# Attention and projection kernel: one query tile projected a step earlier, its key tile spread over slots, and the first value burst one exponential later

## Chip, core and metric

The kernel runs on one core of a Trainium2 chip. The metric is the device time of one execution in microseconds (us); lower is better. Engine names are those of the profile: PE is TensorE's matmuls, PEld its weight loads, DVE is VectorE, ACT is ScalarE, POOL is GpSimd, SP is the engine that issues most of the transfers. ACTq and SPq are the transfers that ACT and SP issue.

## What is computed

There are 16 batches of 512 tokens with 512 features. The first layer is softmax attention with 16 heads of 32 features, the second a linear attention with 8 heads. The change is in the first:

```
xn = layer_norm(x)
q = (xn @ q_w + q_b).reshape(16, 512, 16, 32);  k, v likewise
att = softmax_over_keys(einsum('bnhl,bmhl->bnmh', q, k) + mask)
y = einsum('bnmh,bmhl->bnhl', att, v)
x = x + silu(layer_norm(y) * (1 + scale) + shift) @ out_w + out_b
```

## The kernel before

`attention_phase` does the first layer up to y, `projection_phase` (untouched) all that follows. Attention takes the first 1580 us of the span, in 16 batches of four **steps**. Step g of a batch attends for head group g (four heads, 128 features). A step has 16 **slots** (SLOTS), and the order of work in a slot is written out by hand for each engine, in a function `step` of its own; the engines meet only over semaphores.

What a slot holds on PE, in this order:

1. `exp_scores` (L521), one 100x512 product of scores with keys on the partitions, into one of two `exp_bank`s. ACT takes the exponential of it into `probs` (`exp`, L745). The exponentials run LAG = 3 slots late: slot k of step g does exponential k-3 of this step, slots 0 to 2 do exponentials 13 to 15 of the step before. Product e waits until ACT has done exponential e-2.
2. After product e == 5 (slot 8) stands **burst 1**: `weigh_values` 2 and 3 of the step before (L532) and `sum_probs` (L546). After e == 8 (slot 11) stands **burst 2**: `weigh_values` 0 and 1 of this step. ACT copies y out (`copy_y`) after its exponential 5.
3. `max_scores` (L506), a 98x512 product for the next step into one of two `max_bank`s, whose row maximum DVE reduces into `negmax` (`maximum`, L879). 16 of them stand in slots 0 to 10: one in an even slot, two in an odd one, the second at the slot's end (`maxima`). Maximum m waits until DVE has reduced m-2.
4. Between a slot's first and second maximum, one **quarter** of a projected tile (`project_quarter`, L489: three 128x512 products), or four transposes of x (`transpose_x`, L496) in step 1. QUARTERS gives the slots: q in 0 to 3, k in 4 to 7, the first v in 8 to 11, the second in 13 to 15. Steps 0 and 3 have q, k and two v tiles, step 1 has q, k and x in slots 8, 9, 11, 13, step 2 has q and k alone. The q and k tiles are those of two steps on: steps 2 and 3 project groups 0 and 1 of the next batch.
5. In slot 12 the transpose of `negmax` (L512), whose result SP copies into `q_stack` as two shift rows, which exponential product 0 of the next step waits for (`shift_rows`).

When the last quarter of a q or k tile is done, ACT writes its high part (`high_of`, L719) to a stage and issues two transfers of it into the rows of `q_stack` or `k_stack` (`stack_high`, L726). They stand in ACT's order between two exponentials. DVE then makes the low part (`low_of`, L865) one slot later, and SP issues its transfer. Seven transfers a group count up one semaphore `stack_in[g]`, which PE waits for before the group's first maximum, and ACT before it writes the stage again.

Projections and transposes share two `work_bank`s in turn; `take_bank` waits until the use before the last has been read. `uses_of` is the list of uses in a step in their order.

Of the kernel before, what the change touches and what calls it, by code (L numbers as in the profile page):

```python
# [21 lines left out]
F32 = mybir.dt.float32  # L22
# [6 lines left out]
T = 512  # L29
D = 512  # L30
TT = T // P
KT = D // P
DH0 = 32
HG = P // DH0
NG = KT
# [69 lines left out]
def attention_phase(nc, shared, x, mask, mask1, norm_w, norm_b, q_w, q_b, k_w, k_b, v_w, v_b, cond, films, b_vectors,  # L105
# [4 lines left out]
    with ExitStack() as ctx:  # L110
# [83 lines left out]
        hi_done = sem("hi_done")  # L194
        stack_in = [sem(f"stack_in{g}") for g in range(NG)]
        shift_hi, shift_in = sem("shift_hi"), [sem(f"shift_in{g}") for g in range(NG)]
# [9 lines left out]


        def uses_of(g, last):
            u = []
            if not last or g < NG - 2:  # L210
                u += ["q", "k"]
            if g == 0:
                u += ["v2"]
            if g == 1 and not last:
                u += [f"x{tt}" for tt in range(TT - 1)]
            if g == NG - 1 and not last:
                u += ["v0"]
            if not last or g < NG - 1:
                u += ["m"]
            if g == 1 and not last:  # L220
                u += [f"x{TT - 1}"]
            if g == 0:
                u += ["v3"]
            if g == NG - 1 and not last:
                u += ["v1"]
            return u
# [7 lines left out]
        X_TURNS = (8, 9, 11, 13)  # L234
        MAX_TURN = 12

# [20 lines left out]

        def high_count(b, g, i):

            return TT + 4 + HIGHS * b + (2 * g + (TT if g > 1 else 0)) + i + 1  # L260

        STACK_DMAS = 2 * 3 + 1
        HIGH_ROWS = {"q": (0, 2), "k": (0, 1)}
# [27 lines left out]
        def _(sp):  # L291
# [30 lines left out]
            def mask_rows(b, g):  # L322
                sp.dma_start(k_stack[96:98, g, :, :].bitcast(F32),
                             mb_dram[b].unsqueeze(1).broadcast_to([2, HG, T])).then_inc(stack_in[g], DMA)

            def stack_low(n, g):
                sp.dma_start(stack_rows(n, LOW_ROW[n], g), stage[n][:, 1, :].bitcast(F32)).then_inc(stack_in[g], DMA)

# [37 lines left out]
            def step(b, g, last=False, first=False):  # L366
                if not last or g < NG - 2:
                    s_b, s_g = (b, g + 2) if g + 2 < NG else (b + 1, g + 2 - NG)
                    if not (first and g + 2 < NG):

                        sp.wait_ge(exp_full, SLOTS * (step_of(b, g) - 1))
                    mask_rows(s_b, s_g)
                if not last or g < NG - 2:
                    sp.wait_ge(work_read, use(b, g, "q", last)[1] + 1)
                    stack_low("q", s_g)

                if not last or g < NG - 2:
                    sp.wait_ge(work_read, use(b, g, "k", last)[1] + 1)
                    stack_low("k", s_g)
                if not (first and g == 0):  # L380
                    store_y(b, g - 1) if g else store_y(b - 1, NG - 1)
                if g == 0 and not first:
                    store_sums(b - 1)
                if not last or g < NG - 1:
                    n_b, n_g = (b, g + 1) if g + 1 < NG else (b + 1, 0)
                    shift_rows(n_b, n_g, use(b, g, "m", last)[1] + 1)
                if g == 2 and not last and not (type(b) is int and b + 2 >= B):

                    sp.wait_ge(work_full, use(b, 1, f"x{TT - 1}")[1] + 1)
                    load_x(b + 2)  # L390
# [72 lines left out]
        def _(pe):  # L463
# [189 lines left out]
            def step(b, g, last=False, first=False):  # L653
# [3 lines left out]
                for k in range(SLOTS):  # L657
# [10 lines left out]
                    for name, slots in QUARTERS.items():  # L668
                        if name in "qk":
                            if last and g >= NG - 2:  # L670
                                continue
                            what, tile, u = name, (g + 2) % NG, name
                        elif g == 0 or (g == NG - 1 and not last):
                            tile = (2 if g == 0 else 0) + (name == "v'")
                            what, u = "v", f"v{tile}"
                        else:
                            continue
                        for kt in range(KT):
                            if slots[kt] != k:
                                continue  # L680
                            if name == "q" and kt == 0 and g == 2:

                                pe.wait_ge(work_read, use(b, 1, f"x{TT - 1}")[1] + 1)
                            if kt == 0:
                                banks[name] = take_bank(use(b, g, u, last))
                            project_quarter(what, tile, banks[name], kt, kt == 0, kt == KT - 1)
                    if g == 1 and not last and k in X_TURNS:
# [22 lines left out]
        def _(act):  # L710
# [11 lines left out]
            def stack_high(what, g, highs):  # L722

                act.wait_ge(hi_done, highs)
                for row in HIGH_ROWS[what]:
                    act.dma_start(stack_rows(what, row, g), stage[what][:, 0, :].bitcast(F32)).then_inc(stack_in[g], DMA)  # L726

# [51 lines left out]
            for g in range(2):  # L779
                for what in "qk":  # L780
                    if g == 1:
                        act.wait_ge(stack_in[0], DMA * STACK_DMAS)
                    high_of(what, g, n, n)
                    n += 1
                    stack_high(what, g, n)
# [14 lines left out]
            def step(b, g, last=False, first=False):  # L800
                for k in range(SLOTS):
                    if not (first and g == 0 and k < LAG):
                        exp_slot(*exp_of(b, g, k), first and g == 0)
                    for what in "qk":
                        if k == QUARTERS[what][-1] and (not last or g < NG - 2):

                            p_b, p_g = (b, g + 1) if g + 1 < NG else (b + 1, 0)
                            act.wait_ge(stack_in[p_g], DMA * STACK_DMAS * (p_b + 1))
                            static, number = use(b, g, what, last)
                            high_of(what, (g + 2) % NG, number, static)  # L810
                            stack_high(what, (g + 2) % NG, high_count(b, g, "qk".index(what)))
                    if g == 1 and not last and k in X_TURNS:
# [24 lines left out]
        def _(dve):  # L837
# [167 lines left out]
            def step(b, g, last=False):  # L1005
                has_next = not last or g < NG - 1
                n_b, n_g = (b, g + 1) if g + 1 < NG else (b + 1, 0)
                for k in range(SLOTS):
                    if has_next:
                        for m in maxima(k):  # L1010
                            maximum(n_b, n_g, m)
                    for i, what in enumerate("qk"):
                        if k == QUARTERS[what][-1] + 1 and (not last or g < NG - 2):
                            low_of(what, (g + 2) % NG, use(b, g, what, last)[0], high_count(b, g, i))
                    if g == 1 and not last and 5 <= k < 5 + TT:
                        normalise_x(b + 1, [k - 5])
                    if g == 1 and not last and k - 1 in X_TURNS:
                        tt = X_TURNS.index(k - 1)
                        low_of_x(tt, use(b, 1, f"x{tt}")[0], high_count(b, 1, 2 + tt))
                    if k == 11 and (g == 0 or (g == NG - 1 and not last)):  # L1020
# [781 lines left out]
```

## Time and profile before

| | |
|---|---|
| median of 3 runs | 2839.5 us (2839.39 to 2840.51) |
| the profiled execution's own time | 2837.53 us |
| its span, first to last instruction | 2835.7 us |
| PE busy | 2684.1 us (95%) |
| DVE busy | 1822.6 us (64%) |
| ACT busy | 1228.2 us (43%) |
| POOL busy | 1343.5 us (47%) |

PE is the engine that is nearly always busy. Its matmuls are pipelined: a 512-column matmul is shown as about 0.40 us long, while the next starts 0.23 to 0.24 us after it, so durations are read as the distance from start to start. "Idle before" at a row's end is time in which the engine did nothing, and the name behind the arrow is what it waited for. Runs differ by under 0.1%.

### The profile page before, as it was taken

To read this page: it belongs to the slowest core of one execution; us is meant where nothing else is said; L and a number is where in the kernel's file an instruction comes from. 1 tells how busy PE (TensorE), PEld (TensorE's weight loads), DVE (VectorE), ACT (ScalarE), POOL (GpSimd) and SP (SyncE) were. 2 spreads that over 40 slices of the span, in tenths; PEclk is the share of its full clock that TensorE was granted. 3 is DMA by queue.
4 is the path that set the end of the run, shared out by engine and by line. 5 is a ranking of instruction groups with operands and counts; after the bars stand their busy time and mean duration, and the time that the engine had idled before them with its cause. 6 is when DMAs were issued, how large, how long until landed. Compare 5 with 4: busy or idle time off the path is not lost. (4 is left out here: it accounts for less than half of the span.)

```text
span 2835.7 us, 43874 instructions
## 1 busy us (share of the span) xinstructions
PE 2684.1 (95%) x13890; PEld 1951.8 (69%) x13890; DVE 1822.6 (64%) x3276; ACT 1228.2 (43%) x2040; POOL 1343.5 (47%) x598
## 2 busy tenths in 40 slices
PE   6899999999999999999999689999999999999997
PEld 3565566556655665566555468888888888888886
DVE  4666666666666666666665566777676677666673
ACT  2455555555555555555555423333333333333332
POOL 0365655655666565556566323433333333433332
PEclk9999999999999999999999799999999999999999
DMA  7555656665666566656654411111111111111100
GB/s 181 123 95 95 94 80 94 94 96 78 94 97 98 74 97 98 96 78 96 95 83 69 147 35 49 49 49 45 48 49 45 36 46 41 49 49 35 47 30 30
DMA packets 114915, 211.44 MB, mean 75 GB/s; under 512 B 12408, under 2 KB 14508, under 8 KB 114876
## 3 DMA queue, kind: packets, MB, share of 16 engines
q1 hardware_dynamic: 78012, 143.81, 21.7%
q10 hardware_dynamic: 36864, 67.13, 17.8%
q8 instruction: 22, 0.36, 0.1%
q14 instruction: 17, 0.14, 0.0%
HBM read 74.87 MB, written 34.18 MB: 38 GB/s over the span
## 5 line engine op out<-in xcount | busy, mean ns | idle before, releaser
L879 DVE TENSOR_REDUCE negmax<-max_bank 128x1 f32<-128x512 f32 x1024 | 684.5, 687 | 333.6 <-PE max_bank L506 329.4
L745 ACT ACTIVATE probs<-exp_bank 128x512 f32<-128x512 f32 x1024 | 591.9, 596 | 564.2 <-PE exp_bank L521 469.0
L284 POOL TENSOR_TENSOR probs_sum<-probs_sum,probs 128x2048 f32<-128x2048 f32 x126 | 580.6, 4608 | 86.2 <-ACT probs L745 83.8
L284 POOL TENSOR_TENSOR probs_sum<-probs 128x2048 f32<-128x2048 f32 x63 | 287.9, 4570 | 587.0 <-ACT probs L745 587.0
L506 PE MATMUL max_bank<-k_stack,q_stack 98*128 98x512 f32 x1024 | 426.6, 418 | 27.6 <-DVE negmax L879 22.8
L521 PE MATMUL exp_bank<-q_stack,k_stack 100*128 100x512 f32 x1024 | 422.5, 424 | 23.1 <-ACT probs L745 22.5
L506 PEld LDWEIGHTS max_bank<-k_stack,q_stack 98*128 98x128 f32 x1024 | 195.2, 191 | 149.0 <-issue 58.5
L521 PEld LDWEIGHTS exp_bank<-q_stack,k_stack 100*128 100x128 f32 x1024 | 193.6, 190 | 127.6 <-ACT probs L745 73.1
L1500 POOL TENSOR_TENSOR sT_lo<-silu,sT_hi 128x512 fp32r<-128x512 f32 x128 | 172.8, 1370 | 175.8 <-DVE sT_hi L1615 175.8
L532 PE MATMUL y_bank<-probs,v_sb 128*32 128x512 f32 x2048 | 247.7, 602 | 0.0
L1281 PE MATMUL b_work<-ident,area 128*128 128x128 f32 x1536 | 192.8, 281 | 23.8 <-DMA b_sums<-sums_scratch 12.0
L1255 PE MATMUL b_work<-b_wout_hi,sT_hi 128*128 128x512 f32 x512 | 201.7, 394 | 9.6 <-issue 5.1
L1281 PEld LDWEIGHTS b_work<-ident,area 128*128 128x128 f32 x1536 | 175.9, 145 | 37.9 <-DVE area L1584 13.0
L1255 PE MATMUL b_work<-b_wout_lo,sT_hi 128*128 128x512 f32 x512 | 201.1, 393 | 0.0
L1255 PE MATMUL b_work<-b_wout_hi,sT_lo 128*128 128x512 f32 x512 | 200.9, 392 | 0.0
L1495 POOL TENSOR_TENSOR rstd_y<-var_eps_y,b_minus_half 128x4 f32<-128x4 f32 x32 | 32.7, 1022 | 333.6 <-DVE var_eps_y L1579 333.6
L1615 DVE CAST sT_hi<-silu 128x512 fp32r<-128x512 f32 x128 | 102.2, 820 | 103.5 <-ACT silu L1440 103.5
L1479 ACT ACTIVATE area<-area 128x512 f32<-128x512 f32 x64 | 40.4, 632 | 275.0 <-POOL area L1545 275.0
L1440 ACT ACTIVATE silu<-b_work,film_b,film_a 128x512 f32<-128x512 f32 x128 | 93.0, 775 | 128.7 <-PE b_work L1281 101.5
L874 DVE TENSOR_TENSOR v_sb<-work_bank,v_bias 128x512 f32<-128x512 f32 x64 | 44.2, 691 | 153.8 <-PE work_bank L489 153.8
L1515 POOL TENSOR_TENSOR result<-area,row_out 128x512 f32<-128x512 f32 x64 | 83.1, 1308 | 125.2 <-DMA out_x<-result 125.2
L532 PEld LDWEIGHTS y_bank<-probs,v_sb 128*32 128x32 f32 x2048 | 53.7, 109 | 123.6 <-issue 121.1
(203 smaller groups left out, 5308.6 us busy)
## 6 DMA issues: line engine op xcount, KB each, us to landing
q_stack<-q_stage ACTq DMA_DIRECT2D x128, 256.0 KB
k_stack<-k_stage ACTq DMA_DIRECT2D x128, 256.0 KB
x_sb<-in_x SPq DMA_DIRECT2D x16, 1024.0 KB, 5.4
q_stack<-q_stage SPq DMA_DIRECT2D x64, 256.0 KB
k_stack<-k_stage SPq DMA_DIRECT2D x64, 256.0 KB
yT_scratch<-y_stage SPq DMA_DIRECT2D x64, 256.0 KB
area<-yT_scratch SPq DMA_DIRECT2D x16, 1024.0 KB, 5.3
area<-in_x SPq DMA_DIRECT2D x64, 256.0 KB, 2.8
```

The source lines that it names most:

```text
L284: eng.tensor_tensor(probs_sum[:, :, :], so_far, probs[:, mt, :, :], ALU.add).then_inc(probs_added, 1)
L506: pe.matmul(max_bank[m % 2][:, :], q_stack[0:ROWS_MAX, g, j, nt * P:(nt + 1) * P], k_stack[0:ROWS_MAX, g, j, :], start=True, stop=True).th ...
L521: pe.matmul(exp_bank[k % 2][:, :], k_stack[0:ROWS_EXP, g, j, mt * P:(mt + 1) * P], q_stack[0:ROWS_EXP, g, j, :], start=True, stop=True).th ...
L532: last = pe.matmul(y_bank[DH0 * j:DH0 * (j + 1), :], v_sb[:, mt, P * j + DH0 * g:P * j + DH0 * (g + 1)], probs[:, mt, j, :], start=(mt == ...
L745: act.activation(probs[:, mt, j, :], exp_bank[k % 2][:, :], ACT.Exp).then_inc(exp_done, 1)
L879: dve.tensor_reduce(negmax[:, m:m + 1], max_bank[m % 2][:, :], AXX, ALU.max, negate=True).then_inc(max_done, 1)
L1255: last = pe.matmul(out, lhs(a, kt), rhs(c, kt), start=(kt == 0 and a + c == 0), stop=(kt == KT - 1 and a == 1))
L1281: last = pe.transpose(out[:, i * P:(i + 1) * P], src(i), ident[:, :])
L1440: act.activation(silu[:, kt % SILUS, :], bank(u), ACT.Silu, scale=film_columns(film_a[film], kt, row), bias=film_columns(film_b[film], kt, ...
L1500: pool.tensor_tensor(sT_lo[:, kt, :], silu[:, kt % SILUS, :], sT_hi[:, kt, :].bitcast(F32), ALU.subtract).then_inc(sT_lo_done, 1)
L1515: pool.tensor_tensor(result[:, tt, :], x_sb[:, tt, :], rows["out1"][:, :], ALU.add).then_inc(result_biased, 1)
L1615: dve.tensor_copy(sT_hi[:, kt, :], silu[:, kt % SILUS, :]).then_inc(sT_hi_done, 1)
```

## The change

- The second q tile of the next batch (group 1) moves from step 3, slots 0 to 3, to step 2, slots 8 to 11. It is called `q'` there.
- The k tile of group 1 stays in step 3 but has its quarters in slots 0, 2, 4 and 6, where it had 4 to 7.
- `stack_in` becomes a semaphore for each group and each of q and k (3 and 4 transfers). ACT's wait before it writes a stage is for the same letter's tile in the group in front; PE waits for both before a group's first maximum.
- Burst 1, and ACT's `copy_y`, stand behind exponential 6 (slot 9), where they stood behind exponential 5 (slot 8).
- SP issues the low part of `q'` behind the shift rows of step 2. High and low parts follow the last quarter as before: ACT in slot 11, DVE in slot 12, ahead of `split_shift`.

```diff
+        def tiles_of(g, last):
+            return {n: t for n, t in TILES[g].items() if not last or g == 0 or (g == 1 and n in "qk")}
...
+        TILES = [
+            {"q": (2, (0, 1, 2, 3)), "k": (2, (4, 5, 6, 7)), "v2": (2, (8, 9, 10, 11)), "v3": (3, (13, 14, 15, 15))},
+            {"q": (3, (0, 1, 2, 3)), "k": (3, (4, 5, 6, 7))},
+            {"q": (0, (0, 1, 2, 3)), "k": (0, (4, 5, 6, 7)), "q'": (1, (8, 9, 10, 11))},
+            {"k": (1, (0, 2, 4, 6)), "v0": (0, (8, 9, 10, 11)), "v1": (1, (13, 14, 15, 15))},
+        ]
...
-        QUARTERS = {"q": (0, 1, 2, 3), "k": (4, 5, 6, 7), "v": (8, 9, 10, 11), "v'": (13, 14, 15, 15)}
...
-        STACK_DMAS = 2 * 3 + 1
+        STACK_DMAS = {"q": 3, "k": 3 + 1}
...
                 if m == 0:
-                    pe.wait_ge(stack_in[g], DMA * STACK_DMAS * (b + 1))
+                    for n in "qk":
+                        pe.wait_ge(*copied(n, b, g))
...
                 exp_scores(b, g, e, first)
                 before = (b, g - 1) if g else (b - 1, NG - 1)
-                if e == 5 and not first:
+                if e == 6 and not first:
                     weigh_values(*before, 2)
                     weigh_values(*before, 3)
                     sum_probs(*before)
...
                 exp(b, g, e, first)
-                if e == 5 and not first:
+                if e == 6 and not first:
                     copy_y(*((b, g - 1) if g else (b - 1, NG - 1)))
...
-                    for what in "qk":
-                        if k == QUARTERS[what][-1] and (not last or g < NG - 2):
+                    for name, (tile, slots) in tiles_of(g, last).items():
+                        if name[0] in "qk" and k == slots[-1]:
 
-                            p_b, p_g = (b, g + 1) if g + 1 < NG else (b + 1, 0)
-                            act.wait_ge(stack_in[p_g], DMA * STACK_DMAS * (p_b + 1))
-                            static, number = use(b, g, what, last)
-                            high_of(what, (g + 2) % NG, number, static)
-                            stack_high(what, (g + 2) % NG, high_count(b, g, "qk".index(what)))
+                            act.wait_ge(*copied(name[0], *group_in_front(*stacked(b, g, name))))
+                            static, number = use(b, g, name, last)
+                            high_of(name[0], tile, number, static)
+                            stack_high(name[0], tile, high_count(b, g, name))
```

Where the instructions stand. The first place is the end of step 2 on ACT, in batch 0; `probs` are exponentials, the two DMA rows those of `stack_high`, `y_stage` is `copy_y`. Before:

```order
L719 ACTIVATE k_stage<-work_bank,bias_cols 128x512
L726 DMA k_stack<-k_stage 32x4x512 x2
L745 ACTIVATE probs<-exp_bank 128x512
L752 ACTIVATE y_stage<-y_bank 128x512
L745 ACTIVATE probs<-exp_bank 128x512 x11
L719 ACTIVATE q_stage<-work_bank,bias_cols 128x512
L726 DMA q_stack<-q_stage 32x4x512 x2
```

After:

```order
L725 ACTIVATE k_stage<-work_bank,bias_cols 128x512
L732 DMA k_stack<-k_stage 32x4x512 x2
L751 ACTIVATE probs<-exp_bank 128x512 x2
L758 ACTIVATE y_stage<-y_bank 128x512
L751 ACTIVATE probs<-exp_bank 128x512 x2
L725 ACTIVATE q_stage<-work_bank,bias_cols 128x512
L732 DMA q_stack<-q_stage 32x4x512 x2
L751 ACTIVATE probs<-exp_bank 128x512 x11
```

The q stage and its two transfers stood behind exponential 0 of step 3 (11 exponentials after `copy_y`: 6 to 15 and 0); they now stand behind exponential 8 of step 2, ahead of exponential 9.

The second place is the end of step 2 on PE, from burst 2 to the first maximum of step 3. Before:

```order
L532 MATMUL y_bank<-probs,v_sb 32x512 x8
L521 MATMUL exp_bank<-q_stack,k_stack 128x512
L512 MATMUL work_bank<-ident,negmax 16x128
L521 MATMUL exp_bank<-q_stack,k_stack 128x512 x4
L506 MATMUL max_bank<-k_stack,q_stack 128x512
```

After:

```order
L547 MATMUL y_bank<-probs,v_sb 32x512 x8
L503 MATMUL work_bank<-xT_hi,wq_hi 128x512
L503 MATMUL work_bank<-xT_lo,wq_hi 128x512
L503 MATMUL work_bank<-xT_hi,wq_lo 128x512
L536 MATMUL exp_bank<-q_stack,k_stack 128x512
L527 MATMUL work_bank<-ident,negmax 16x128
L536 MATMUL exp_bank<-q_stack,k_stack 128x512 x4
L521 MATMUL max_bank<-k_stack,q_stack 128x512
```

The last quarter of `q'` stands ahead of exponential products 9 to 13; behind it nothing has changed.

The third place is the beginning of step 3 on PE. Before:

```order
L506 MATMUL max_bank<-k_stack,q_stack 128x512
L489 MATMUL work_bank<-xT_hi,wq_hi 128x512
L489 MATMUL work_bank<-xT_lo,wq_hi 128x512
L489 MATMUL work_bank<-xT_hi,wq_lo 128x512
L506 MATMUL max_bank<-k_stack,q_stack 128x512
L521 MATMUL exp_bank<-q_stack,k_stack 128x512
L506 MATMUL max_bank<-k_stack,q_stack 128x512
L489 MATMUL work_bank<-xT_hi,wq_hi 128x512
L489 MATMUL work_bank<-xT_lo,wq_hi 128x512
L489 MATMUL work_bank<-xT_hi,wq_lo 128x512
L521 MATMUL exp_bank<-q_stack,k_stack 128x512
```

After:

```order
L503 MATMUL work_bank<-xT_hi,wk_lo 128x512
L536 MATMUL exp_bank<-q_stack,k_stack 128x512
L521 MATMUL max_bank<-k_stack,q_stack 128x512 x2
L536 MATMUL exp_bank<-q_stack,k_stack 128x512
L521 MATMUL max_bank<-k_stack,q_stack 128x512
L503 MATMUL work_bank<-xT_hi,wk_hi 128x512
L503 MATMUL work_bank<-xT_lo,wk_hi 128x512
L503 MATMUL work_bank<-xT_hi,wk_lo 128x512
L536 MATMUL exp_bank<-q_stack,k_stack 128x512
```

A quarter stood between the two maxima of every odd slot; now an odd slot has none, and its two maxima and the next slot's stand with one exponential product among them.

## Rows read from the trace of the kernel before

**Rows 1.** The page: one engine's busy time, and the costliest group of instructions.
```profile
PE 2684.1 (95%) x13890; PEld 1951.8 (69%) x13890; DVE 1822.6 (64%) x3276; ACT 1228.2 (43%) x2040; POOL 1343.5 (47%) x598
...
L879 DVE TENSOR_REDUCE negmax<-max_bank 128x1 f32<-128x512 f32 x1024 | 684.5, 687 | 333.6 <-PE max_bank L506 329.4
```

**Rows 2.** Windows: length, busy PE, PEld, DVE, ACT, POOL; granted clock, DMA share, GB/s.
```profile
681.50:703.20 21.70, 19.64 (x109) 11.76 (x108) 16.17 (x27) 12.93 (x24) 12.28 (x6) 1.00 0.61 85
703.20:724.30 21.10, 19.72 (x98) 11.40 (x97) 12.45 (x20) 11.18 (x20) 13.80 (x4) 1.00 0.63 87
724.30:750.10 25.80, 25.47 (x128) 17.05 (x127) 14.32 (x23) 12.52 (x23) 16.49 (x4) 1.00 0.64 115
...
608.70:631.20 22.50, 21.11 (x98) 12.50 (x98) 12.43 (x20) 11.17 (x20) 13.65 (x4) 0.93 0.59 82
608.30:611.70 3.40, 3.40 (x9) 2.64 (x9) 1.12 (x2) 1.39 (x3) 3.40 (x1) 0.50 0.02 7
```

**Rows 3.** Timeline of PE, batch 6, step 2: start, length, instruction, idle before.
```profile
713.26 0.40 PE L521 MATMUL exp_bank<-q_stack,k_stack 100*128 100x512 f32 x1
...
716.31 0.50 PE L506 MATMUL max_bank<-k_stack,q_stack 98*128 98x512 f32 x1
...
716.88 0.39 PE L506 MATMUL max_bank<-k_stack,q_stack 98*128 98x512 f32 x1
717.59 0.50 PE L506 MATMUL max_bank<-k_stack,q_stack 98*128 98x512 f32 x1 [0.32 <-DVE negmax L879]
...
718.85 0.51 PE L506 MATMUL max_bank<-k_stack,q_stack 98*128 98x512 f32 x1 [0.51 <-DVE negmax L879]
...
719.52 1.92 PE L532 MATMUL y_bank<-probs,v_sb 128*32 128x512 f32 x16
721.37 0.50 PE L521 MATMUL exp_bank<-q_stack,k_stack 100*128 100x512 f32 x1
...
723.75 0.50 PE L521 MATMUL exp_bank<-q_stack,k_stack 100*128 100x512 f32 x1 [0.20 <-ACT probs L745]
```

**Rows 4.** Timeline of ACT in the same step.
```profile
713.23 0.69 ACT L719 ACTIVATE k_stage<-work_bank,bias_cols 128x512 fp32r<-128x512 f32 x1 [0.20 <-PE work_bank L489]
713.95 1.21 ACTq L726 DMA_DIRECT2D k_stack<-k_stage  x2
715.27 0.60 ACT L745 ACTIVATE probs<-exp_bank 128x512 f32<-128x512 f32 x1 [1.35 <-issue]
...
721.91 2.97 ACT L745 ACTIVATE probs<-exp_bank 128x512 f32<-128x512 f32 x5 [1.53 <-PE exp_bank L521]
```

**Rows 5.** Timeline of PE, batch 6, step 1, slots 8 to 11.
```profile
690.23 0.39 PE L521 MATMUL exp_bank<-q_stack,k_stack 100*128 100x512 f32 x1
690.55 1.92 PE L532 MATMUL y_bank<-probs,v_sb 128*32 128x512 f32 x16
...
693.26 0.50 PE L506 MATMUL max_bank<-k_stack,q_stack 98*128 98x512 f32 x1
...
694.27 0.40 PE L506 MATMUL max_bank<-k_stack,q_stack 98*128 98x512 f32 x1
695.20 0.66 PE L496 MATMUL work_bank<-ident,x_sb 128*128 128x128 f32 x4 [0.53 <-DVE k_stage L865]
...
696.91 1.92 PE L532 MATMUL y_bank<-probs,v_sb 128*32 128x512 f32 x16
```

**Rows 6.** Timeline of PE, batch 6, step 3, slots 0 to 11.
```profile
724.08 0.40 PE L506 MATMUL max_bank<-k_stack,q_stack 98*128 98x512 f32 x1
724.32 0.40 PE L489 MATMUL work_bank<-xT_hi,wq_hi 128*128 128x512 f32 x1
...
734.32 0.40 PE L521 MATMUL exp_bank<-q_stack,k_stack 100*128 100x512 f32 x1
...
741.26 1.07 PE L532 MATMUL y_bank<-probs,v_sb 128*32 128x512 f32 x8
```

**Rows 7.** DMA issues from 230 to 1500 us: count, KB each, median us to landing.
```profile
q_stack<-shift SPq DMA_DIRECT2D x110, 8.0 KB, 1.9
```

More of the change, by code:

```diff
@@ L194, in attention_phase @@
         hi_done = sem("hi_done")
-        stack_in = [sem(f"stack_in{g}") for g in range(NG)]
+        stack_in = {n: [sem(f"{n}_stack_in{g}") for g in range(NG)] for n in "qk"}
         shift_hi, shift_in = sem("shift_hi"), [sem(f"shift_in{g}") for g in range(NG)]
@@ L202, in attention_phase @@
         sums_full, sums_read, sums_stored = sem("sums_full"), sem("sums_read"), sem("sums_stored")
+        def tiles_of(g, last):
+            return {n: t for n, t in TILES[g].items() if not last or g == 0 or (g == 1 and n in "qk")}
         def uses_of(g, last):
[L209 to L213, printed above, removed]
+            at = [(slots[0], n) for n, (_, slots) in tiles_of(g, last).items()]
             if g == 1 and not last:
-                u += [f"x{tt}" for tt in range(TT - 1)]
-            if g == NG - 1 and not last:
-                u += ["v0"]
+                at += [(k, f"x{tt}") for tt, k in enumerate(X_TURNS)]
             if not last or g < NG - 1:
[L219 to L226, printed above, removed]
+                at.append((MAX_TURN, "m"))
+            return [n for _, n in sorted(at)]
+        TILES = [
[4 rows of a table added]
+        ]
+        X_TURNS = (8, 9, 11, 13)
+        MAX_TURN = 12
         FIRST_USES = [f"x{tt}" for tt in range(TT)] + ["q0", "k0", "q1", "k1", "m", "v0", "v1"]
@@ L256, in attention_phase, with high_count, stacked, copied @@
         HIGHS = 2 * NG + TT
-        def high_count(b, g, i):
-            return TT + 4 + HIGHS * b + (2 * g + (TT if g > 1 else 0)) + i + 1
-        STACK_DMAS = 2 * 3 + 1
+        def high_count(b, g, what):
+            highs = [n for h in range(g) for n in uses_of(h, False) if n[0] in "qkx"]
+            here = [n for n in uses_of(g, False) if n[0] in "qkx"]
+            return TT + 4 + HIGHS * b + len(highs) + here.index(what) + 1
+        def stacked(b, g, name):
+            group = TILES[g][name][0]
+            return (b, group) if group > g else (b + 1, group)
+        def copied(n, b, g):
+            return (stack_in[n][g], DMA * STACK_DMAS[n] * (b + 1))
+        def group_in_front(b, g):
+            return (b, g - 1) if g else (b - 1, NG - 1)
+        STACK_DMAS = {"q": 3, "k": 3 + 1}
         HIGH_ROWS = {"q": (0, 2), "k": (0, 1)}
@@ L366, in step, with low_in @@
             def step(b, g, last=False, first=False):
-                if not last or g < NG - 2:
-                    s_b, s_g = (b, g + 2) if g + 2 < NG else (b + 1, g + 2 - NG)
-                    if not (first and g + 2 < NG):
+                tiles = tiles_of(g, last)
+                if "k" in tiles:
+                    s_b, s_g = stacked(b, g, "k")
+                    if not (first and g < 2):
                         sp.wait_ge(exp_full, SLOTS * (step_of(b, g) - 1))
                     mask_rows(s_b, s_g)
[L373 to L379, printed above, removed]
+                def low_in(name):
+                    sp.wait_ge(work_read, use(b, g, name, last)[1] + 1)
+                    stack_low(name[0], stacked(b, g, name)[1])
+                for name in "qk":
+                    if name in tiles:
+                        low_in(name)
                 if not (first and g == 0):
@@ L667, in step @@
                             transpose_max(n_b, n_g, use(b, g, "m", last))
[L668 to L677, printed above, removed]
+                    for name, (tile, slots) in tiles_of(g, last).items():
                         for kt in range(KT):
@@ L684, in step @@
                             if kt == 0:
-                                banks[name] = take_bank(use(b, g, u, last))
-                            project_quarter(what, tile, banks[name], kt, kt == 0, kt == KT - 1)
+                                banks[name] = take_bank(use(b, g, name, last))
+                            project_quarter(name[0], tile, banks[name], kt, kt == 0, kt == KT - 1)
                     if g == 1 and not last and k in X_TURNS:
@@ L725, in stack_high @@
                 for row in HIGH_ROWS[what]:
-                    act.dma_start(stack_rows(what, row, g), stage[what][:, 0, :].bitcast(F32)).then_inc(stack_in[g], DMA)
+                    act.dma_start(stack_rows(what, row, g), stage[what][:, 0, :].bitcast(F32)).then_inc(stack_in[what][g], DMA)
             def mask_value(b, mt, number):
@@ L781, in _ @@
                     if g == 1:
-                        act.wait_ge(stack_in[0], DMA * STACK_DMAS)
+                        act.wait_ge(*copied(what, 0, 0))
                     high_of(what, g, n, n)
@@ L1011, in step @@
                             maximum(n_b, n_g, m)
-                    for i, what in enumerate("qk"):
-                        if k == QUARTERS[what][-1] + 1 and (not last or g < NG - 2):
-                            low_of(what, (g + 2) % NG, use(b, g, what, last)[0], high_count(b, g, i))
+                    for name, (tile, slots) in tiles_of(g, last).items():
+                        if name[0] in "qk" and k == slots[-1] + 1:
+                            low_of(name[0], tile, use(b, g, name, last)[0], high_count(b, g, name))
                     if g == 1 and not last and 5 <= k < 5 + TT:
```

11 lines of the change are left out of this document (6 added, 5 removed).

## Prediction, made before the changed kernel ran

> **What bounds the kernel now.** I read the page first: PE is busy 95% of the span, DVE with its row maxima far less, but a maximum takes it 687 ns [rows 1], and PE's own matmul only 0.24 us from start to start (724.08 to 724.32 [rows 6]). So work that only changes its place on PE costs or gains nothing by itself; what counts are the places where PE waits. Next the windows of three steps of batch 6 [rows 2]: step 1 takes 21.7 us, step 2 21.1, step 3 25.8, with 19.6, 19.7 and 25.5 of PE busy. Steps 1 and 2 have the slack, step 3 hardly any. Then the timeline of PE says where. In step 2 maximum 14 waits 0.32 us and maximum 15 0.51 us for DVE [rows 3]; the reader is to see that from maximum 12 to 14 it is 1.28 us (716.31 to 717.59) and from 13 to 15 1.97, while PE had one or two matmuls to do in between. **1.28 us is the least distance between a maximum and the next but one**: two banks, and DVE must have reduced the earlier. Behind burst 2 PE has exponential products alone, which ACT paces: product 9 starts at 721.37, product 13 at 723.75, 2.38 us for four starts worth 0.24 each [rows 3]. In step 1 the second transpose of x waits 0.53 us for DVE's low part of k, which sits behind maximum 12, which sits behind burst 1 [rows 5].
>
> **The change part by part.** A batch has one such change in each of steps 1 to 3; batches 0 to 14 have all of them (15 times), batch 15 projects nothing in steps 2 and 3.
>
> *Burst 1 behind exponential 6, step 1.* From product 5 to burst 2 it is 6.68 us now (690.23 to 696.91 [rows 5]). After: product 5, 0.24; maximum 12, the transposes and product 6, 1.01 (693.26 to 694.27) less the 0.10 by which a matmul behind a burst starts later, 0.91; burst 1, 2.71 (690.55 to 693.26); then maximum 13 and, at the least distance, 15, 1.28; from 15 to burst 2 0.67 (718.85 to 719.52 [rows 3]). Sum 5.81: **-0.87 us**. The wait of the second transpose is gone, since maximum 12 and the low part of k now pass while PE does burst 1. Steps 0 and 3, full of quarters, show no wait around burst 1 and gain nothing from it.
>
> *`q'` in step 2, slots 8 to 10.* From product 5 to burst 2 it is 6.26 us now (713.26 to 719.52 [rows 3]). With three quarters among them PE does just what step 3 does there, 6.94 us (734.32 to 741.26 [rows 6]), in either order of the burst. **+0.68 us** for nine matmuls worth 2.1: both waits for DVE are filled. This is what the slack of step 2 gives.
>
> *`q'` in step 2, slot 11 and after.* The last quarter stands behind burst 2: three matmuls, 0.82 us with the slow first, the last starting 0.58 us after the burst's end. Only now can ACT act, and it has the stage and **two transfers to issue ahead of exponential 9**. How long that is, the k tile shows: its last matmul starts at about 712.80 (two matmuls before 713.26), ACT writes the stage from 713.23 for 0.69, issues from 713.95 for 1.21, and begins its next exponential at 715.27, with 1.35 us idle put down to issue [rows 4]. That is 2.47 us from matmul to exponential. For k it costs nothing, since burst 1 covers it; behind burst 2 there is no cover: PE has products 9 and 10 and the small transpose, and then both banks are full. Exponential 9 begins 0.58 + 2.47 = 3.05 us after the burst. From there PE's product 13 follows as now, 723.75 - 721.91 = 1.84 [rows 3, 4]. So 4.89 us where 2.38 stood: **+2.51 us**, of which 0.7 is work. Step 2 in all: +3.19 for a tile worth 2.83 (12 matmuls of 0.236).
>
> The Trainium skill speaks on the issue: DMA: Bandwidth & Descriptors, section Issuing engines are not separate DMA queues, says that initiating a DMA takes the initiating sequencer a time "which is usually small relative to the DMA itself". By the row it is 1.21 us for two; by that rule, taken as nothing, the tail would be 1.35 shorter and the sum 20 us lower. The row decides, and ACT's lost time is at the worst place.
>
> The shift rows also hang on this tail: DVE makes the low part of `q'` (about 0.7, as a maximum) ahead of `split_shift`. Stage at 1.0 to 1.7 us, low part to 2.5, split to 3.1, SP's issue and 1.9 us to land [rows 7]: there by about 6.3 us after the burst, while product 0 stands about 8.5 after it (4.89, then three slots). Cover for 2 us; without it, each microsecond would count. Taken as 0. The split semaphores cost nothing: what they count has landed long before either wait, and each is one more wait instruction. SP's low part of `q'` behind the shift rows is needed only at the end of the next step but one: 0.
>
> *Step 3 without its q tile.* PE loses 12 matmuls, 2.83 us. But quarters no longer stand in the odd slots. There the order is now maximum b, maximum c, product, maximum a, quarter, product, maximum b again. From b to a PE has three starts, 0.71 us; the least distance is 1.28: a wait of 0.57, and the matmul behind it starts 0.10 late (0.34 after it, as after 717.59). Then three matmuls of a quarter and a product: b to b is 1.28 + 0.34 + 4 x 0.235 = 2.56 us where 8 matmuls would be 1.87. Four such pairs, up to maximum 12: it stands 10.14 us after maximum 0. Then 0.34 + 0.71 for the first v quarter; product 6 at 11.19, but it needs exponential 4, and ACT has k's stage and two transfers ahead of that (k now ends in slot 6, its last matmul at 8.4; 8.4 + 2.47 + 0.65 for the exponential and its signal = 11.5). Burst 1 at 11.85, and it lasts 2.71. What is left to burst 2 is what followed burst 1 before (6.94 - 0.33 - 2.71 = 3.90) without maximum 12, a quarter and product 6 (1.28) and with 0.10 for the start behind a burst: 2.72. Sum 17.3 from maximum 0 to burst 2, where it is 17.18 now (724.08 to 741.26 [rows 6]): **+0.1 us**. The whole tile that is taken out goes into waits for maxima. Bounds: -2.83 if no maximum waits, +0.1 as worked out; I take +0.1, as the same three starts between maxima 12 and 14 cost 1.28 in [rows 3].
>
> *Batch 15:* steps 1 and 2 with no tile in slots 8 to 11 gain 0.8 and 0.6 by the burst: -1.4.
>
> *The clock.* In batch 5 step 2 took 22.5 us, not 21.1, with a granted clock of 0.50 of 2.4 GHz, which is 1.2, for 608.3 to 611.7 [rows 2], right behind the thin end of step 1. The new end of step 2 is thinner: from product 10 PE has nothing for over 2 us. A fall there costs 0 to 1.4 us a batch (22.5 less 21.1), and part of the slow stretch falls on waits: I take 0.7.
>
> **The sum:** 15 x (-0.87 + 0.68 + 2.51 + 0.1) = +36.3; batch 15 -1.4; clock 15 x 0.7 = +10.5. Together +45. The profiled execution took 2837.5 us itself, so 2882.9; the median of the runs shown is 2.0 above it: **2885 us**, 1.6% slower.
>
> **The rivals.**
> *Step 3 gives its tile back* (faster): if DVE's reductions caught up so that no maximum in slots 0 to 7 waits, step 3 has -2.83 and the batch -0.87 + 3.19 - 2.83 = -0.51; with no fall of the clock 2839.5 - 7.7 - 1.4 = 2830. For it: DVE is busy only 14.3 of 25.8 us in step 3 [rows 2]. Against it: the wait is for one reduction, not for DVE's load. It decides once more than 2.4 of the 2.9 us come back. If also the issue on ACT were hidden (-1.8 more), 2803. Chance of this side 0.10.
> *It evens out:* step 3 gives back most of its tile and the clock takes it again: 2839 within 5. Chance 0.05.
> *Half:* one of the two new waits at half its size (step 3 gives 1.4 back, or the tail costs 1.3 less), no clock: 2854 to 2858. Slower still. Chance 0.15.
> *More:* the clock falls in each batch at full price, and the thin step 3 costs more restarts: 2896 to 2905. Chance 0.15.
> *The forecast*, 2865 to 2895: 0.55.
> *The change does nothing* can't be: steps 2 and 3 have another order on three engines.
>
> **The numbers.** 0.2%, 5.7 us, is about what a measurement of this kernel can tell. Slower by more: 0.55 + 0.15 + 0.15, 0.85. Within: 0.05. Faster: 0.10. The range leaves out the faster rival and little else: 2852 to 2904; that of the likeliest case alone is 2865 to 2895.
>
> **What would show it.** In the profile after: in step 2, 1.35 us of ACT idle for issue behind the q stage in slot 11, and then a wait of PE's product 11 of about 2 us for ACT; no wait for DVE at maxima 14 and 15; in step 3 four waits of about 0.57 us for `negmax`; in step 1 no wait for `k_stage`; step 2 near 24.3 us, step 3 near 25.9, step 1 near 20.8. I am wrong if product 11 follows product 10 within a microsecond, if step 3's maxima are reduced in time, or if product 0 of step 3 waits for the shift rows, which would come on top.

## The result, and the profile after

The changed kernel takes 2897.8 us (median of 4 runs, 2887.5 to 2903.2) against 2839.6: a ratio of 1.020, with a 95% interval of 1.017 to 1.023. It is slower, as forecast. That is 13 us more than the 2885 that was predicted: inside the whole range (2852 to 2904), but above the likeliest case (2865 to 2895), where the rival "More" stood. Its runs differ by 16 us among themselves; those of before differ by 1 here, and by 7 over all 33 taken in the study.

The page after, to be read beside [rows 1]. PE is busy 36 us longer over a span that is 66 us longer, with the same matmuls: part of the loss is idle time, part is matmuls at the lower clock.

```profile
span 2901.4 us, 43958 instructions
...
PE 2720.2 (94%) x13890; PEld 1971.0 (68%) x13890; DVE 1822.1 (63%) x3276; ACT 1229.9 (42%) x2040; POOL 1342.6 (46%) x598
```

The windows answer to [rows 2]: steps 1, 2 and 3 of batch 6, step 3 of batch 3, and a stretch at the beginning of batch 6's step 3, where the clock was at its lower level (length, busy PE, PEld, DVE, ACT, POOL, granted clock, DMA share, GB/s).

```profile
706.20:727.80 21.60, 19.76 (x110) 11.99 (x109) 16.19 (x27) 13.01 (x25) 12.39 (x6) 1.00 0.62 86
727.80:752.10 24.30, 21.95 (x110) 13.74 (x109) 13.12 (x21) 11.87 (x21) 13.82 (x4) 1.00 0.66 95
752.10:779.00 26.90, 25.21 (x116) 15.40 (x115) 13.59 (x22) 11.82 (x21) 16.30 (x4) 0.94 0.52 93
457.90:484.40 26.50, 24.13 (x116) 14.49 (x116) 13.58 (x22) 11.89 (x22) 16.44 (x4) 1.00 0.52 95
752.50:755.90 3.40, 3.40 (x9) 2.20 (x8) 1.98 (x4) 1.35 (x3) 3.40 (x1) 0.51 1.07 122
```

Where the clock did not fall, step 1 went from 21.7 to 21.5, step 2 from 21.1 to 24.3, and step 3, which gave a whole tile away, from 25.8 up to 26.5. Step 0 is unchanged at 24.5. Both sides of the move lost.

The tail of step 2 on PE, behind burst 2, and then on ACT. It answers to [rows 3] and [rows 4]:

```profile
744.77 1.92 PE L547 MATMUL y_bank<-probs,v_sb 128*32 128x512 f32 x16
746.62 0.50 PE L503 MATMUL work_bank<-xT_hi,wq_hi 128*128 128x512 f32 x1
746.96 0.40 PE L503 MATMUL work_bank<-xT_lo,wq_hi 128*128 128x512 f32 x1
747.20 0.40 PE L503 MATMUL work_bank<-xT_hi,wq_lo 128*128 128x512 f32 x1
747.44 0.39 PE L536 MATMUL exp_bank<-q_stack,k_stack 100*128 100x512 f32 x1
747.67 0.27 PE L527 MATMUL work_bank<-ident,negmax 128*16 128x128 f32 x1
747.70 0.47 PE L536 MATMUL exp_bank<-q_stack,k_stack 100*128 100x512 f32 x1
750.33 0.99 PE L536 MATMUL exp_bank<-q_stack,k_stack 100*128 100x512 f32 x2 [2.16 <-ACT probs L751]
751.52 0.50 PE L536 MATMUL exp_bank<-q_stack,k_stack 100*128 100x512 f32 x1 [0.20 <-ACT probs L751]
```

```profile
747.64 0.69 ACT L725 ACTIVATE q_stage<-work_bank,bias_cols 128x512 fp32r<-128x512 f32 x1 [2.01 <-PE work_bank L503]
748.36 1.21 ACTq L732 DMA_DIRECT2D q_stack<-q_stage  x2
749.68 2.98 ACT L751 ACTIVATE probs<-exp_bank 128x512 f32<-128x512 f32 x5 [1.35 <-issue]
```

ACT's first exponential behind the burst starts 2.48 us after the last matmul of `q'` (747.20 to 749.68); product 13 stands 4.90 us behind the burst (746.62 to 751.52). The prediction had 2.47 and 4.89.

Step 3 on PE, slots 2 to 9 of batch 3, where the clock is whole. It answers to [rows 6]:

```profile
460.08 0.50 PE L521 MATMUL max_bank<-k_stack,q_stack 98*128 98x512 f32 x1 [0.31 <-DVE negmax L884]
...
461.64 0.50 PE L536 MATMUL exp_bank<-q_stack,k_stack 100*128 100x512 f32 x1 [0.35 <-DMA q_stack<-shift]
...
463.16 0.50 PE L521 MATMUL max_bank<-k_stack,q_stack 98*128 98x512 f32 x1 [0.33 <-DVE negmax L884]
...
465.61 0.50 PE L521 MATMUL max_bank<-k_stack,q_stack 98*128 98x512 f32 x1 [0.33 <-DVE negmax L884]
...
468.06 0.50 PE L521 MATMUL max_bank<-k_stack,q_stack 98*128 98x512 f32 x1 [0.32 <-DVE negmax L884]
...
469.67 0.49 PE L536 MATMUL exp_bank<-q_stack,k_stack 100*128 100x512 f32 x1 [0.41 <-ACT probs L751]
```

Four waits for a maximum, the wait for exponential 4 behind k's issue, and one that the prediction had taken as nothing: product 0 waits for the shift rows. From batch 1 to 14 this wait shows in only two steps, the two in which the clock was whole; in the other twelve PE was slowed and came to product 0 later. The transfers say how it arises: SP's two shift transfers behind step 2, first in the kernel before, then in the changed one (time from issue to landing).

```profile
L333 SPq DMA_DIRECT2D q_stack<-shift x2: 579/585/591, 722.6 to 723.3; - x2
...
DMA to landing us min/median/max: 2.1/2.2/2.3
```

```profile
L343 SPq DMA_DIRECT2D q_stack<-shift x2: 580/583/586, 749.6 to 750.3; - x2
...
DMA to landing us min/median/max: 5.4/5.5/5.5
```

It is so in all 14 batches: 2.1 to 2.4 us before, 5.4 to 5.6 after.

Step 1 on PE, slots 8 to 11, and what DVE does there. It answers to [rows 5]:

```profile
714.99 0.39 PE L536 MATMUL exp_bank<-q_stack,k_stack 100*128 100x512 f32 x1
715.68 0.50 PE L521 MATMUL max_bank<-k_stack,q_stack 98*128 98x512 f32 x1 [0.30 <-DVE negmax L884]
...
716.79 1.92 PE L547 MATMUL y_bank<-probs,v_sb 128*32 128x512 f32 x16
...
721.46 1.92 PE L547 MATMUL y_bank<-probs,v_sb 128*32 128x512 f32 x16
```

```profile
713.03 0.95 DVE L859 TENSOR_SCALAR x_sb<-x_sb,mv,rstd 128x512 f32<-128x512 f32 x1
713.90 0.68 DVE L884 TENSOR_REDUCE negmax<-max_bank 128x1 f32<-128x512 f32 x1
714.50 0.53 DVE L859 TENSOR_SCALAR x_sb<-x_sb,mv,rstd 128x512 f32<-128x512 f32 x1
714.96 1.27 DVE L884 TENSOR_REDUCE negmax<-max_bank 128x1 f32<-128x512 f32 x2
```

From product 5 to burst 2 it is 6.47 us, where 6.68 stood and 5.81 was expected. The wait for `k_stage` is gone. But DVE also normalises the next batch's x in these slots, 0.5 to 0.95 us a tile, and is behind; burst 1 used to hide that from maximum 12, which now waits. From product 5 to burst 1 it is 1.80 us (714.99 to 716.79), where 1.15 was counted (0.24 + 0.91); behind that everything is as predicted.

### The profile page after: what moved, and what is told of

It reads as the page before. It is cut to its first block and busy times, and to the rows that moved or that the text cites. A ratio compares the mean times of both kernels' runs of the same rounds, so it can differ in the third digit from the quotient of the medians.

```text
span 2901.4 us, 43958 instructions
## 1 busy us (share of the span) xinstructions
PE 2720.2 (94%) x13890; PEld 1971.0 (68%) x13890; DVE 1822.1 (63%) x3276; ACT 1229.9 (42%) x2040; POOL 1342.6 (46%) x598
## 5 line engine op out<-in xcount | busy, mean ns | idle before, releaser
L536 PE MATMUL exp_bank<-q_stack,k_stack 100*128 100x512 f32 x1024 | 431.9, 434 | 54.3 <-ACT probs L751 52.3
L1286 PE MATMUL b_work<-ident,area 128*128 128x128 f32 x1536 | 192.8, 280 | 24.9 <-DMA b_sums<-sums_scratch 13.1
```

What stands on the lines that cost most here:

```text
L536: pe.matmul(exp_bank[k % 2][:, :], k_stack[0:ROWS_EXP, g, j, mt * P:(mt + 1) * P], q_stack[0:ROWS_EXP, g, j, :], start=True, stop=True).th ...
L1286: last = pe.transpose(out[:, i * P:(i + 1) * P], src(i), ident[:, :])
```

## The experiments

"Clean" below is the median length of a step, over those of batches 1 to 14 in which the granted clock did not fall, read as the windows above. Clean steps of one kernel agree within about 0.1 us but for batch 1, so one profiled execution is enough for them; the whole time also has the clock in it. A step is cut at the start of its exponential 13 on ACT. At the ends of steps 3 and 0 that is 1.3 us later behind PE's maximum 0 than at the other two, since ACT has a v tile to finish first: from maximum 0 to maximum 0, steps 1 and 3 of the kernel before take PE 23.0 and 24.5 us, not 21.7 and 25.8. The offset is the same in both kernels, so the differences stand. A wait "a step" is the idle time in front of such rows, averaged over the same 14 steps. The clean steps 0 to 3 are 24.5, 21.7, 21.1, 25.8 before and 24.5, 21.5, 24.3, 26.5 after. Of the changed kernel's steps 2 and 3 only two each are clean (24.30 and 24.30; 26.46 and 26.48).

**Burst 1 alone moved.**

```diff
--- before
-                if e == 5 and not first:
+                if e == 6 and not first:
                     weigh_values(*before, 2)
...
-                if e == 5 and not first:
+                if e == 6 and not first:
                     copy_y(*((b, g - 1) if g else (b - 1, NG - 1)))
```

> The kernel before with burst 1 and copy_y behind exponential 6 and nothing else. By the prediction's own term step 1 loses 0.87 us and step 2 0.8, together about 25 us over the run. By what the trace after shows, maximum 12 of step 1 is no longer hidden by the burst, so step 1 goes from 21.7 to 21.5 only, and step 2 from 21.1 to about 20.3: 15 x 1.0 + 1.4, 16 us faster than before, near 2823. Rival: the burst's place is worth nothing, 2839.

Measured: 2814.7 us, ratio 0.991 (0.990 to 0.993). The windows of steps 1 to 3 of batch 6:

```profile
670.20:691.70 21.50, 19.65 (x109) 11.86 (x108) 16.20 (x27) 12.92 (x25) 12.29 (x6) 1.00 0.62 86
691.70:712.00 20.30, 19.46 (x98) 11.46 (x97) 12.43 (x20) 11.08 (x20) 13.78 (x4) 1.00 0.64 87
712.00:737.80 25.80, 25.47 (x128) 17.10 (x127) 14.32 (x23) 12.54 (x23) 16.51 (x4) 1.00 0.65 118
```

The steps are as expected, but the gain is 25 us, not 16. The rest is the clock: from batch 1 to 14 it fell in 7 batches before, each time where step 1 ends, and in none here. Yet the two waits at that end are still there (batch 6):

```profile
689.32 0.66 PE L496 MATMUL work_bank<-ident,x_sb 128*128 128x128 f32 x4 [0.84 <-DVE xT_lo L860]
...
691.15 0.50 PE L521 MATMUL exp_bank<-q_stack,k_stack 100*128 100x512 f32 x1 [0.71 <-ACT probs L745]
```

What has changed in step 1 lies ahead of them, in slots 8 to 10: the burst, the wait of 0.53 us for `k_stage`, which is gone, and one of 0.3 us for maximum 12, which has come. **This part of the change is good, and with it alone the kernel is the fastest of the study that computes everything**, faster than both. The tile moves cost 83 us on top of it.

**The tile moves alone** (the changed kernel with both `e == 6` back at `e == 5`).

> The changed kernel with burst 1 and copy_y back behind exponential 5, so the two tile moves and the semaphores alone. Theory: step 1 is back at 21.7; step 2 stays near 24.3 (its tail behind burst 2 is untouched); step 3 loses about 0.9 us, since burst 1 again covers the wait of maximum 12 (0.45) and the wait of the next product for exponential 4 (0.5): 25.6 where the changed kernel has 26.5. Rival, that the moved burst is part of the loss in every step: step 2 below 24.

Measured: 2899.6 us (one run). Step 1 is 21.7 and step 2 24.3, clean. Step 3 has no clean one; its shortest is 25.7 with a fall in it, so it is no longer than that. The profile's waits for DVE in step 3 go from 1.07 us a step to 0.64 and the one for ACT is gone. As the theory has it, as far as a step with a fall can show. The whole is no faster than the changed kernel; the clock fell 24 times, not 18.

**The q transfers issued by SP.**

```diff
--- after
+                            if name != "q'":
-                            stack_high(name[0], tile, high_count(b, g, name))
+                                stack_high(name[0], tile, high_count(b, g, name))
...
                 if "q'" in tiles:
+                    sp.wait_ge(hi_done, high_count(b, g, "q'"))
+                    for row in HIGH_ROWS["q"]:
+                        sp.dma_start(stack_rows("q", row, 1), stage["q"][:, 0, :].bitcast(F32)).then_inc(stack_in["q"][1], DMA)
                     low_in("q'")
```

> The changed kernel with the two transfers of the high part of q' issued by SP behind the shift rows, where ACT issued them ahead of exponential 9. Theory of the issue on ACT: product 11 of step 2 waits 1.3 us less for ACT, step 2 goes from 24.3 to 23.0; the shift rows now go out ahead of the q' transfers, so the wait of product 0 of step 3 for them (0.35) is gone as well, step 3 26.0. Rival: the tail is set by the stage and the exponentials, not by the issue: step 2 stays at 24.3.

Measured: 2862.2 us (one run), 36 faster than the changed kernel. Step 2 is 22.8 clean, step 3 25.9. PE and ACT at the end of step 2 of batch 7, and the shift transfers of batch 6:

```profile
824.68 0.47 PE L539 MATMUL exp_bank<-q_stack,k_stack 100*128 100x512 f32 x1
825.85 0.98 PE L539 MATMUL exp_bank<-q_stack,k_stack 100*128 100x512 f32 x2 [0.69 <-ACT probs L754]
```

```profile
824.62 0.69 ACT L728 ACTIVATE q_stage<-work_bank,bias_cols 128x512 fp32r<-128x512 f32 x1 [2.00 <-PE work_bank L506]
825.21 2.96 ACT L754 ACTIVATE probs<-exp_bank 128x512 f32<-128x512 f32 x5
```

```profile
L343 SPq DMA_DIRECT2D q_stack<-shift x2: 579/583/587, 732.0 to 732.6; - x2
...
DMA to landing us min/median/max: 1.8/1.9/1.9
```

ACT goes from the stage straight to the exponentials, the wait shrinks from 2.16 to 0.69 us, and the shift rows land in 1.9 us again. Both are one cause: two transfers issued by ACT at the wrong moment. They hold up ACT for 1.35 us, and they put the small shift transfers behind 512 KB of traffic. This run changes both the issuing engine and the order, so it does not say whether the order alone would help the shift rows.

**The k quarters in odd slots** (`"k": (1, (1, 3, 5, 7))` in the changed kernel).

> The changed kernel with the k quarters of step 3 in slots 1, 3, 5, 7, where it has 0, 2, 4, 6. Theory of the least distance of about 1.2 us between a maximum and the next but one: a quarter stands between an odd slot's two maxima again, so each pair of slots takes about 2.25 us, not 2.45, and step 3 goes from 26.5 to about 25.7. Rival: DVE has too little time for 12 maxima in any case and the place of the quarters does not matter: 26.5.

Measured: 2885.9 us (one run); step 3 is 25.4 clean. PE in batch 7, product 0 and maxima 5, 8 and 11:

```profile
847.06 0.50 PE L536 MATMUL exp_bank<-q_stack,k_stack 100*128 100x512 f32 x1 [1.46 <-DMA q_stack<-shift]
...
848.33 0.40 PE L521 MATMUL max_bank<-k_stack,q_stack 98*128 98x512 f32 x1
...
850.54 0.40 PE L521 MATMUL max_bank<-k_stack,q_stack 98*128 98x512 f32 x1
...
852.75 0.40 PE L521 MATMUL max_bank<-k_stack,q_stack 98*128 98x512 f32 x1
```

A pair of slots takes 2.21 us (848.33 to 850.54) where the changed kernel has 2.45 (465.61 to 468.06). Eight matmuls alone would take 1.87, so some of the wait for DVE is left. Part of the gain is lost again at once: the shorter slots bring product 0 forward, and in a clean step it waits 1.46 us for the shift rows.

**PE kept busy in the wait.**

```diff
--- after
+                    if g == 2 and k == 13 and not last:
+                        for _ in range(28):
+                            pe.transpose(max_bank[0][0:SLOTS, 0:P], negmax[:, :], ident[:, :])
```

> The changed kernel with 28 extra 128-column transposes on PE in step 2, behind product 10, where PE waits 2.16 us for ACT anyway; they write a maximum bank that nobody reads then, so the output is the same. They take about 1.6 us of that wait. Theory that the thin end of step 2 makes the granted clock fall and that this costs about 0.9 us a batch: the falls behind step 2 are gone, steps 2 and 3 show 24.3 and 26.5 in every batch, the whole is 10 to 15 us faster than the changed kernel, near 2885. Rival: the falls have another cause, or cost nothing: as the changed kernel, 2898, or slower by the added work.

Measured: 2888.7 us (median of 4, 2887.5 to 2892.9), ratio to before 1.019 (1.017 to 1.020). **With 28 useless matmuls more in 15 steps it is not slower than the changed kernel, and 9 us faster by the medians.** The changed kernel's own runs are 16 us apart and the shortest is 2887.5, so the times alone would not settle it; the clean steps and the falls do. The transposes took 3 us, more than the wait, so step 2 is 0.6 longer (24.9 clean, 9 us over the run). Step 3 was never slowed: 14 of 14 are clean, where the changed kernel has 2, and the falls from batch 1 to 14 go from 18 to 5. Those behind step 2 go from 12 to none; the 5 that are left stand behind step 1, as 6 of the 18 did. The mean batch is 1.1 us shorter. Step 3 is 25.9, since product 0 comes later and no longer waits for the shift rows.

**Half of each maximum**, in the kernel before and in the changed one (`max_bank[m % 2][:, 0:256]` in `maximum`; the maximum is over half of the scores, part of the computation is left out).

> The kernel before, with each row maximum in the attention taken over 256 of the 512 scores: the subtracted maximum is another one, so part of the computation is left out. A reduction takes about 0.4 us, not 0.69. This is the partner of the next run. Theory: the two waits of step 2 for DVE go (step 2 from 21.1 to about 20), step 3, which has none, stays at 25.8.

Measured: 2813.0 us (one run); step 1 is 21.3, step 2 20.5, step 3 25.8, and the clock did not fall from batch 1 to 14.

> The changed kernel with the same half maxima (256 of 512 scores, part of the computation left out). Theory of the wait for a reduction in step 3: the four waits for maxima shrink from about 0.45 to under 0.2 us each, so step 3 goes from 26.5 to about 25.2, while the same cut does nothing to step 3 of the kernel before. What is left above 25.8 - 2.8 = 23.0 is then the wait for the exponential behind k's issue and for the shift rows. Step 2 stays at 24.3, since its tail does not wait for DVE. Rival, that step 3 is bound by ACT or by the transfers: it stays at 26.5.

Measured: 2887.9 us (one run). Step 2 stays at 24.3. The waits of step 3 for DVE go from 1.07 us a step to 0.03, and a pair of slots from 2.45 to 2.17. But step 3 is 26.3 at its shortest, always with a fall of the clock in it, not 25.2: its wait for exponential 4 grew from 0.41 to 0.69. The rows show the wait for DVE for what it was; of what step 3 would be without it and without a fall, this run gives no number. With the falls, the mean of 14 steps goes from 27.2 to 26.5. Step 1 is 20.8 here, just what the prediction had for it, where it is 21.5 with whole maxima: what it is short of there is DVE's time.

**The quarters of `q'` ahead of burst 2** (`"q'": (1, (8, 9, 9, 10))` in the changed kernel).

> The changed kernel with the quarters of q' in slots 8, 9, 9, 10, where they were in 8 to 11: all ahead of burst 2. Theory of the uncovered issue: ACT's stage and its two transfers now run beside burst 2 (1.85 us), product 11 waits about 0.5 us and not 2.2, step 2 takes about 22.4; the shift rows land in time, step 3 about 26.0; hardly a fall of the clock; about 2850 in all, still slower than before. Rival, that it is the added tile itself that makes step 2 long: 24.3.

Measured: 2887.0 us (one run). Step 2 is 22.8 clean, as the theory of the cover has it. **Step 3 is 27.2 (two clean steps), the longest of all, which I had wrong**, and with it the 2850 for the whole. PE's product 0 and the transfers it waited for:

```profile
751.21 0.50 PE L536 MATMUL exp_bank<-q_stack,k_stack 100*128 100x512 f32 x1 [1.21 <-DMA q_stack<-shift]
```

```profile
L343 SPq DMA_DIRECT2D q_stack<-shift x2: 578/584/591, 744.8 to 745.5; - x2
...
DMA to landing us min/median/max: 4.4/5.1/5.7
```

Of the 1.5 us that the shorter tail gave back, the shift rows took half (0.7): they still land 4.4 to 5.7 us after their issue, behind the q transfers, and PE, no longer held up in the tail, comes to product 0 before them.

**All of it mended**: `q'` in slots 8, 9, 9, 10, its high part issued by SP behind the shift rows, k in slots 1, 3, 5, 7.

> The changed kernel with every cost mended that the runs so far have shown: q' ends ahead of burst 2 (slots 8, 9, 9, 10), SP issues its high part behind the shift rows, and k has the odd slots 1, 3, 5, 7 of step 3. Theory: step 2 near 22.6, step 3 near 25.0, with steps 0 and 1 at 24.5 and 21.5: 93.6 us a batch without falls of the clock, where the kernel before has 93.1 and the kernel with the burst alone 92.1. So about 2835, the same as before within half a per cent, and slower than the burst alone: the tile is worth no more in step 2 than in step 3. Rival, that the tile move pays once its waits are gone: under 2815.

Measured: 2821.0 us, ratio to before 0.994 (0.992 to 0.996); I had expected 2835.

```profile
694.90:717.40 22.50, 21.95 (x110) 13.69 (x109) 13.19 (x21) 11.79 (x21) 13.85 (x4) 1.00 0.59 83
717.40:741.40 24.00, 23.44 (x116) 14.74 (x116) 13.59 (x22) 11.81 (x22) 16.43 (x4) 1.00 0.67 123
```

Step 3 gives back 1.8 of its 2.8 us and is better than I expected by one; step 2 takes 1.4 more than before. Against the burst alone, 24.5 + 21.5 + 20.3 + 25.8, it is 92.5 to 92.1 us a batch, and 2821.0 to 2814.7 in all: the move itself is still worth nothing beside the other half of the change. Its waits for the issue and the shift rows are gone; that for the maxima is smaller, not gone, since a pair of slots takes 2.2 us as in the run with odd slots. Whether the move pays without that rest is not shown.

**PE kept busy in the kernel before** (12 such transposes in step 1, slot 13, ahead of the wait for x's low part).

> The kernel before with 12 extra 128-column transposes on PE in step 1, slot 13, in the 0.84 us in which it waits for the low part of x; they write a maximum bank that nobody reads then, so the output is the same. Theory of the clock: the falls behind step 1, which make step 2 take 22.5 and not 21.1 in every second batch, are gone, worth 7 x 1.4 = 10 us, less up to 0.1 us a batch that the transposes may add: 2830. Then 10 of the 25 us that the burst alone gains are the clock's. Rival: the falls are not from this idle stretch, 2839.

Measured: 2831.5 us, ratio 0.998 (0.997 to 0.999). Step 1 is 22.0, 0.3 longer (4 us over the run), step 2 is 21.1 in all batches but one. From batch 1 to 14 one fall is left of 7, so the falls behind step 1 cost about 10 us in the kernel before, and filling its last idle stretch is enough to be rid of them. It is not needed for that: with the burst alone this stretch was as idle (0.84 and 0.71 us), and no fall came. So the idle stretch alone does not decide, and what does is open.

## Why the prediction was right, and what it missed

The direction was right, and so were the mechanisms in step 2 (the issue on ACT without cover) and step 3 (the order of the maxima). Two terms were put too low, by 10 and 9 us over the run. By its time alone the result lies in the rival "More" (2896 to 2905, chance 0.15), but not by its mechanism: the clock did not cost its full price of 1.4 us a batch.

*The tail of step 2*, +2.51 us: right to 0.01 in the profile, and its cause shown by taking it away (SP issuing: step 2 from 24.3 to 22.8) and by covering it (quarters ahead of burst 2: 22.8). The Trainium skill's sentence that the time to initiate a DMA is "usually small relative to the DMA itself" (DMA: Bandwidth & Descriptors, Issuing engines are not separate DMA queues) is not contradicted: these transfers land 4.2 to 5.7 us after their issue, which itself takes 0.6 us each. But it does not help an engine on which the issue stands in front of awaited work.

*Slots 8 to 10 of step 2*, +0.68: right. With the tail, step 2 was to be 3.19 longer and is 3.2.

*Burst 1*, -0.87 in step 1: **four times too large**, -0.21 was measured. The step that failed is "maximum 12, the transposes and product 6 ... 0.91", which took the maximum as free of waits since burst 1 was its only neighbour. DVE's normalising of x stands ahead of it. With half maxima, which leave DVE time, step 1 is the 20.8 that was predicted. That the burst's place does nothing in steps 0 and 3 was right, as was -0.8 in a step 2 without a tile, seen in the kernel with the burst alone.

*Step 3*, +0.1: +0.7 was measured. The waits for maxima are there, four times, with 2.45 us a pair instead of 2.56; the wait for exponential 4 is there with 0.41. What was mis-sized is the shift rows: "there by about 6.3 us after the burst ... Cover for 2 us". I took their 1.9 us to land from a trace in which nothing large was issued ahead of them. Behind the two transfers of `q'` they take 5.5 us, and the pair of slots with product 0 in it takes 3.08 us (460.08 to 463.16), where the next two take 2.45. I had named that wait as one that would come on top, but not asked what the moved step's own transfers do to those behind it. In the two runs in which product 0 no longer waits for them, by SP's issue and by the transposes, step 3 is the 25.9 that was predicted.

*The clock*, +0.7 us a batch: about right, though it was a guess between 0 and 1.4. In the profiled execution the mean batch is 1.66 us over the clean one (98.43 to 96.77), where before it is 0.84 (93.91 to 93.07): +0.8. That the thin tail causes the falls behind step 2 is shown by the run that fills it: 12 falls become none. The others, behind step 1, were there before.

The sum of the measured terms: 15 x (-0.2 + 3.2 + 0.7 + 0.8) = +67.5, less 1 for batch 15, to be held against the 65.7 us between the two spans. The forecast had +45: 10 too little in step 1, 9 in step 3. The median of the runs is 5 below the profiled one, and the runs are 16 us apart. They go in order with the mean granted clock on record for each: 2887.5 us at 0.975, 2894.2 at 0.972, 2901.5 at 0.969, 2903.2 at 0.968. The profiled execution is the one with the lowest clock.

The rival "step 3 gives its tile back" failed on the order within a pair of slots, as worked out. With that order mended, and the transfers, 1.8 of 2.8 us do come back (24.0). The rival "Half" was put at 2854 to 2858; its own terms give 2853 to 2855, which changes nothing.

## What to carry to other kernels

A step that is moved takes its evacuation and its transfers along: look for what is queued behind them on the issuing engine at the new place, and what small transfer now lands behind their bytes. A long matmul burst behind the issue covers the issue; it did nothing for the small transfer, which had to be issued ahead of the large ones. Where two buffers alternate, spread the filler between each use and the next but one; bunching it left PE idle here, though DVE was busy for only 13.6 of 26.5 us. Test the parts of a change apart: here one of them made the kernel 25 us faster, and the rest then 83 us slower.

## What was not expected of the hardware

- Two 8 KB transfers land in 1.8 to 2.4 us in the kernel before, and in 5.4 to 5.6 us in the changed one, where two 256 KB transfers were issued 1.3 us ahead of them by another engine.
- Useless matmuls in a wait can make a kernel faster, because the granted clock does not fall to 0.5 (1.2 of 2.4 GHz) behind it. In the kernel before, 12 in each of 15 steps gained 7 us (interval 3 to 9), although each of these steps was 0.3 us longer, and 7 falls became one. In the changed kernel, 28 in each of 15 steps took away all 12 falls behind them.
- The same two waits of PE, 0.84 and 0.71 us at the end of step 1, were followed by a fall in every second batch before and by none with the burst moved, where what differs in that step is the work and the waits of slots 8 to 10. Why is not shown.
